# One unit of each image moved behind the first part of the next half, and a DMA queue reordered, in a fused attention and bottleneck kernel

## What is computed

```python
k = conv(x, w1, dilation=2, padding=6) + b1       # 256 -> 128 channels
k = conv(k, w2) + b2                              # 128 -> 49, 1 x 1
attn = softmax(k, axis=1)
x = einsum('bkchw,bkhw->bchw', shifts(x), attn)
```

## Time and profile before

| | |
|---|---|
| median of three runs | 887.78 us (887.29 to 890.51) |
| the profiled execution | 886.85 us |
| its span in the trace | 884.6 us |
| TensorE (PE) busy | 813.1 us, 92% |
| VectorE (DVE) busy | 648.6 us, 73% |
| ScalarE (ACT) busy | 376.6 us, 43% |
| GpSimd (POOL) busy | 358.4 us, 41% |
| mean granted TensorE clock | 0.98 of full |
| SyncE's queue, share of 16 DMA engines | 62.7% |

### The profile page before, as it was taken

One profiled execution on the slowest core, in us unless ns is written; L12 is line 12 of the kernel. 1 busy time (PEld: TensorE's weight loads), 2 busy tenths in 40 slices (PEclk: granted clock), 3 DMA queues, 4 the chain that ended last, 5 costly groups with the idle time before them and its releaser, 6 DMA issues.

```text
span 884.6 us, 13933 instructions
## 1 busy us (share of the span) xinstructions
PE 813.1 (92%) x5084; PEld 769.1 (87%) x5084; DVE 648.6 (73%) x864; ACT 376.6 (43%) x647; POOL 358.4 (41%) x276
## 2 busy tenths in 40 slices
PE   4988988999999999999999999999977989997796
PEld 4988987999999999999999999999967867775685
DVE  4786898887698688769868876886475667228796
ACT  1332212344334433434443343444255689116397
POOL 3757587375267247526624752662200010005300
PEclk9999999999999999999999999999989989998999
DMA  9920415987895998789598887658399986011498
GB/s 262 380 84 1 88 35 123 211 219 167 182 203 134 238 158 218 162 186 212 127 244 155 213 186 169 166 129 229 72 240 265 248 295 286 0 44 51 161 426 364
DMA packets 249420, 162.18 MB, mean 183 GB/s; under 512 B 191321, under 2 KB 232266, under 8 KB 246666
## 3 DMA queue, kind: packets, MB, share of 16 engines
q1 hardware_dynamic: 240650, 144.52, 62.7%
q10 hardware_dynamic: 8704, 16.78, 6.5%
HBM read 99.48 MB, written 56.36 MB: 176 GB/s over the span
## 4 chain that ended last, share of the span: by engine, by line
PE 67%; DVE 11%; issue 6%; ACT 4%; POOL 4%; SPq 4%; DMA 2%; ACTq 0%; DVEq 0%; POOLq 0%
PE ps L1079 19%; PE ps L1081 19%; PE ps L1080 18%; PE ps L1149 4%; PE ps L1165 3%; PE ps L1197 3%; DVE whole L1459 2%; SPq L586 2%; POOL xbuf L772 2%; DVE wsum L1432 2%; DVE wpart L1432 2%; POOL ring L761 2%; PE ps L1104 1%; DMA w1raw<-in_L_conv_w 1%; DVE y L1762 1%
## 5 line engine op out<-in xcount | busy, mean ns | idle before, releaser
L761 POOL TENSOR_TENSOR ring<-whole,ring 128x576 fp32r<-128x576 f32 x112 | 180.6, 1617 | 264.8 <-ACT ring L853 264.8
L1079 PE MATMUL ps<-w_hi,ring 128*128 128x336 f32 x832 | 276.7, 333 | 10.6 <-DVE me L1539 4.5
L1081 PE MATMUL ps<-w_hi,ring 128*128 128x336 f32 x832 | 264.6, 318 | 0.0
L1080 PE MATMUL ps<-w_lo,ring 128*128 128x336 f32 x832 | 263.2, 316 | 0.0
L1079 PEld LDWEIGHTS ps<-w_hi,ring 128*128 128x128 f32 x832 | 159.0, 191 | 11.9 <-issue 9.0
L1080 PEld LDWEIGHTS ps<-w_lo,ring 128*128 128x128 f32 x832 | 158.8, 191 | 0.0
L1081 PEld LDWEIGHTS ps<-w_hi,ring 128*128 128x128 f32 x832 | 157.9, 190 | 0.0
L853 ACT ACTIVATE ring<-whole 128x576 fp32r<-128x576 f32 x112 | 87.2, 780 | 96.3 <-POOL whole L756 51.6
L853 ACT ACTIVATE band_hi<-ps 128x320 fp32r<-128x320 f32 (+1 forms) x128 | 53.3, 419 | 137.8 <-PE ps L1149 131.2
L1079 PE MATMUL ps<-band_hi,xT_hi 128*128 128x224 f32 (+2 forms) x320 | 95.2, 297 | 9.4 <-DVE band_lo L1392 9.3
L1080 PE MATMUL ps<-band_lo,xT_hi 128*128 128x224 f32 (+2 forms) x320 | 92.9, 290 | 0.0
(11 more groups left out here) (165 smaller groups left out, 1375.5 us busy)
## 6 DMA issues: line engine op xcount, KB each, us to landing
xq<-in_x SPq DMA_DIRECT2D x116, 256.0 KB, 5.4
raw<-bands SPq DMA_DIRECT2D x32, 768.0 KB, 7.3
xbuf<-in_x SPq DMA_DIRECT2D x16, 1024.0 KB, 8.7
x_dram<-x ACTq DMA_DIRECT2D x32, 512.0 KB, 4.4
x1in<-x_dram SPq DMA_DIRECT2D x7, 2048.0 KB, 13.3
bands<-wide SPq DMA_DIRECT2D x32, 398.0 KB, 6.2
out<-x1in SPq DMA_DIRECT2D x12, 1024.0 KB, 6.4
w1raw<-in_L_conv_w SPq DMA_DIRECT2D x2, 3136.0 KB, 12.7
```

The costliest lines, as they stand in the source:

```text
L761: pool.tensor_tensor(split(k, 1), positions(whole[:, k % TBUFS, :], 0, 2), split(k, 0).bitcast(F32), ALU.subtract).then_inc(sig_lo_done, 1)
L1079: pe.matmul(dst, l_hi, r_hi_, start=first, stop=False, **kw)
L1080: pe.matmul(dst, l_hi, r_lo_, start=False, stop=False, **kw)
L1081: return pe.matmul(dst, l_lo, r_hi_, start=False, stop=last, **kw)
```

## The change

Unit 9 of images 0 to 11 moves on TensorE from the end of its half into part 1 of the next, behind the transposes of band tile 0 and half of the first chunk; in the last half (image 12) it stays. ScalarE's `x_hi(tail, 1)` and `x_out(tail, 1)` go from part 0 to part 1, VectorE's `x_lo(tail, 1)` from part 2 to part 3. On SyncE `store_y(tail)` goes behind `load_xq(image, 3)` and `scatter(soft)`; and in halves with a softmax `load_raw(coming, 0)` goes ahead of `load_xq(coming, 0)`.

```diff
--- before.py
+++ after.py
@@ -649,18 +649,22 @@
                     load_xq(image, 2)
                 if q % 2 == 1 and conv is not None:
                     load_x(2 * conv + XBUFS)
-                if tail is not None:
-                    store_y(tail)
                 if image is not None:
                     load_xq(image, 3)
                 if soft is not None:
                     scatter(soft)
+                if tail is not None:
+                    store_y(tail)
                 if q % 2 == 1 and conv is not None:
                     load_x(2 * conv + 1 + XBUFS)
                     spill(conv, 1)
                     if q == 2 * PAIRS - 1:
                         spill(conv, 0)
-                if coming is not None:
+                if coming is not None and soft is not None:
+
+                    load_raw(coming, 0)
+                    load_xq(coming, 0)
+                elif coming is not None:
                     load_xq(coming, 0)
                     load_raw(coming, 0)
                 if q == 2 * PAIRS - 1:
@@ -965,7 +969,7 @@
             def half(q):
                 conv, first, image, tail, coming, soft = schedule(q)
                 for part in range(2 * SLOTS + 1):
-                    if part == 0 and tail is not None:
+                    if part == 1 and tail is not None:
                         x_hi(tail, 1)
                         x_out(tail, 1)
                     if part == 6 and tail is not None:
@@ -1233,12 +1237,15 @@
                 if part == 14:
                     unit(image, 6)
                     proj(image, 0)
-                    for i in (7, 8, 9):
+
+                    for i in (7, 8) if image < DRAIN - 1 else (7, 8, 9):
                         unit(image, i)
 
             def half(q):
                 conv, first, image, tail, coming, soft = schedule(q)
                 for part in range(2 * SLOTS + 1):
+                    if part == 1 and tail is not None:
+                        unit(tail, 9)
                     if part == 5 and tail is not None:
                         proj(tail, 1)
                     if image is not None:
@@ -1641,7 +1648,7 @@
                             image_part(image, i)
                             if i in (9, 12) and q == 2 * PAIRS - 1:
                                 (softmax_top if i == 9 else softmax_end)(conv)
-                    if part == 2 and tail is not None:
+                    if part == 3 and tail is not None:
                         x_lo(tail, 1)
                     if conv is not None:
                         for i in combos.get(part, ()):
```

## The result

The changed kernel took 891.34 us in the median of 20 runs (886.65 to 897.22), the kernel before 888.22 us in 20 runs (886.01 to 892.07). The ratio is 1.0031, with an interval of 1.0018 to 1.0044: slightly slower, and within the 0.5% that the prediction called no change. The forecast was 887.1 us, and its range, 881.5 to 890.0, was too low. It had the place of the new wait right, its sum 1.7 us too small, and no price for the clock. Of the 4.2 us between forecast and median, 0.4 come from the kernel before, whose median was 887.78 in the three runs known then.

A forecast was written before the change was run, and what follows sets the result against it. The prediction took TensorE as the bound, with only its gaps to win. Term 1 won 0.65 us, terms 2 and 3 cost 0, taking the profiled 886.85 us to 886.2 and the median 887.78 to 887.1; range 881.5 to 890.

The forecast's parts named there:

- Term 1: TensorE at six odd-half ends: a raw-load wait of 1.33 us replaces band_lo's 1.55; 0.65 us won in all.
- the sign to watch for: TensorE's waits after odd halves: band_lo's 9.3 us gone, a raw wait six times, 7 to 9 us in all.
- one wait of 2.05 us: Sixth odd end: the raw load lands at 572.89, so TensorE's sequence begins 0.5 us later than before.
- Terms 2 and 3: SyncE's reordered queue in even halves, and the later copies behind unit 9: both covered by spare time, cost 0.
- The chain behind unit 9: ScalarE's and VectorE's later copies after even halves: x_lo ends near 236.7, projection at 238.08, 1.4 us to spare, cost 0.
- too few buffers: Skill page's reading of the repeating TensorE gap, by which reordering would win 0; the trace bore it out only in part.
- Full gain: Rival at odd ends: the raw load is not awaited, all 9.3 us are won, 878.5 us; chance 0.14.
- Half the gain: Rival at six ends: raw lands 0.5 to 1 us sooner, 3 to 6 us won, 881.8 to 884.8; chance 0.08.
- Slower by the x rows of even halves: Rival: swapped xq loads land late for x transposes, 1.9 us at five even ends, 9.5 us, 897; chance 0.12.

The follow-up runs named there:

- e4: The change with the first raw load of odd halves put ahead of the spill (except in the last half): 877.09 us, ratio 0.9873 to the kernel before.
- e2: The kernel before with only the change's edits on SyncE, unit 9 in its old place: 888.42 us, ratio 1.0005 to the kernel before.
- e8: The change with odd halves' first raw load ahead of the spill, but the old SyncE queue in even halves: 877.5 us, ratio 0.9872 to before.
- e1: The change without its edits on SyncE, so only unit 9 and its copies move: 889.74 us, ratio 1.0016 to the kernel before.
- e6: The change with the first raw load of odd halves put behind the second xq pair: 915.38 us, ratio 1.030 to the kernel before.
- e3: The change with the first raw load ahead of the first xq pair in odd halves too: 877.09 us, ratio 0.9877 to the kernel before.
- e7: The change with half of the first convolution chunk ahead of band tile 0's transposes on TensorE: 878.66 us, ratio 0.988 to the kernel before.
- e9: e4 with image 14's two raw loads ahead of that image's last two xq pairs in the drain: 879.42 us, ratio 0.9897 to the kernel before.

## Why the prediction was right and wrong

**What bounds the kernel.** Right: TensorE in the steady stage, by its gaps alone. e4 takes out the gaps and is 11 us faster.

**Term 1, the move.** The step was right in its mechanism: band_lo's wait gone, the raw load's in its place, because the odd half's queue stays. Three of six waits were within 0.1 us of the 1.33 forecast. It failed in size. The term took one landing, 7.4 us, as if it were a constant, and gave it 0.3 us of error to both sides. The landings that matter in the change were 7.4 (twice), 7.5 and 8.6, and 6.6 and 7.3 at the two ends where the load goes out later behind its spill. The wait for a transfer is one-sided: a late landing is paid in full, an early one wins at most the wait. Six waits came to 10.44 us, where the term had 5 x 1.33 + 2.05 = 8.7, and the sign to watch for was 7 to 9. At the six ends of the kernel before, the landings were 6.3, 7.4, 7.5, 7.4, 7.4 and 7.1, so the same place gave no hint of 8.6; but all its 22 raw loads from 170 to 600 us landed after 5.7 to 9.1. This error alone would have made the forecast 888.8, still inside the range.

**The clock was missing from the term.** No step priced what a longer wait does to the matmuls behind it. This is the step that failed: the sum has only the waits themselves, and the clock's price at nothing. The prediction had itself worked out one wait of 2.05 us. After the wait of 2.50 us the stretch took 1.5 us more, and after the one of 2.23 us TensorE did 127 matmuls in 20 us, where it does 137 to 138, so 1.5 us again. In the steady stage of the kernel before no wait was over 1.59 us, and none had a slower clock behind it. The waits are 1.7 us over the term and the clock 1.5 + 1.5 us; with the drain's wait, 6.1 against 4.2, that is 6.6 us over the 886.2 forecast for one execution, where 6.2 were measured (892.37). The drain's wait goes with none of the edits: it was 6.5 and 6.0 us in e2 and e8, 4.4 and 4.6 in e1 and e4, 3.8 in e6. Without it the waits and the clock put the median at 887.1 + 1.7 + 3.0 = 891.8, and 891.34 was measured. That the other 19 executions lost as much to waits and clock isn't shown, since one alone was traced. Their recorded mean clocks point that way: of the 20, the six at 0.975 or less have a median of 894.0 us, the 14 at 0.976 or more one of 889.4.

**Terms 2 and 3, cost 0.** Right. The even halves have no wait, and e2 against before and e8 against e4 show no price of the queue beyond 0.2%. The chain behind unit 9 came out close: x_lo ended at 234.85 + 1.28 = 236.1 (236.7 forecast, on a scale 0.4 us earlier), and the projection started at 237.68 without a wait:

```profile
234.85 1.28 DVE L1399 TENSOR_TENSOR x_lo<-ps,x_hi 128x512 fp32r<-128x512 f32 x2
...
240.60 0.69 DVE L1399 TENSOR_TENSOR xT_lo<-ps,xT_hi 128x512 fp32r<-128x512 f32 x1 [0.65 <-ACT xT_hi L857]
```

VectorE's idle time ahead of that xT_lo shrank from 1.66 to 0.65 us: it did take up the delay. The prediction asked whether the repeating gap came from too few buffers, as the Trainium skill's page Perfetto Trace Analysis (Optimization Strategy) says that it can. Here it didn't: e3, e4 and e7 close it by order alone, with the same buffers, and win 10 to 11 us where that reading gave 0.

**The rivals.** Full gain: 878.5 was the right price for a kernel whose raw load isn't awaited (e4: 877.09), and wrong for this one. Half the gain: x rows 3 leave earlier, and raw landed no sooner for it. Slower by the x rows of even halves: didn't happen. The slower case that did happen wasn't among them: a wait at the same place, with a landing that varies and a slower clock behind it.

**The range.** The upper end, 890.0, lay below the slowest run of before that was known, 890.51. A change that takes away the cover of up to 1 us at six places should have moved that end up, by a few us. The chances, 0.7 for within 0.5%, fit the ratio; in this the forecast of "no change" was right, though the way it moved, 0.7 us faster, was not.

## What to carry to other kernels

Before moving work away from behind a wait, look for the transfer that landed in its shadow: the landing time beside the new place of its use tells whether one wait only takes the place of the other. Then the fix is often a place in the issuing queue: here one load, put ahead of a spill it didn't depend on, turned a change of +0.3% into -1.3%. And give a load more cover than its usual landing needs, since a wait pays every late landing in full, and a long one (from 2.2 us on in nine cases of ten here) in clock too.

## What was not expected of the hardware

A longer gap in TensorE's work can have a second price. In 20 us windows from the odd ends, the granted clock was 1.00 behind each wait up to 1.66 us. Behind 2.50, 2.23 (both in the change), 2.20 (e1) and all six of e6, 3.62 to 4.39 us, it was 0.91 or lower. Behind one of 2.47 us in e1 it stayed at 1.00. The windows behind 1.66, 2.50 and 2.23 us in the change:

```profile
186.88:206.88 20.00, 20.00 (x138) 19.76 (x139) 16.57 (x23) 9.38 (x18) 15.67 (x9) 1.00 0.52 139
...
341.84:361.84 20.00, 20.00 (x127) 19.76 (x128) 16.05 (x21) 8.28 (x16) 11.73 (x8) 0.91 0.52 136
...
574.84:594.84 20.00, 20.00 (x127) 19.76 (x128) 16.06 (x21) 8.26 (x16) 12.02 (x8) 0.91 0.52 136
```

and behind 2.47 us in e1:

```profile
574.47:594.47 20.00, 20.00 (x137) 19.77 (x138) 17.32 (x22) 9.38 (x18) 13.25 (x9) 1.00 0.53 136
```

So the length alone doesn't settle it between 2.2 and 2.5 us, and what else does stays open. The finer windows show a short fall to the lower level, 1.2 GHz, and back. Behind the first wait of e6 a whole window lies at 0.50:

```profile
189.64:193.00 3.36, 3.36 (x13) 3.36 (x14) 1.66 (x2) 0.36 (x1) 0.99 (x1) 0.50 0.37 99
```

Behind the wait of 2.50 us in the change the fall begins a little later and spans two windows in part:

```profile
341.84:345.00 3.16, 3.16 (x17) 3.16 (x18) 3.13 (x4) 0.36 (x1) 2.77 (x2) 0.72 0.91 244
345.00:348.00 3.00, 3.00 (x18) 3.00 (x18) 0.90 (x1) 1.95 (x4) 0.00 (x0) 0.73 0.40 123
348.00:351.00 3.00, 3.00 (x23) 2.99 (x22) 1.44 (x3) 1.72 (x4) 1.03 (x1) 1.00 1.06 266
```

The times of the change also spread over 10.6 us in 20 runs, where the kernel before spread over 6.1. Less cover, through which the loads' variation reaches the total, would do that, but it isn't shown: e4, with much cover, spread over 2.8 us in 4 runs, and e9, with the same cover, over 6.8 in 6.
